# Sums of W2 blocks on GpSimd, and the second tile's row statistics taken later, in a three-stage Perceiver block

## The reference

```
# 1 cross attention
attn = softmax(x1 @ ctx^T); attn /= 1e-9 + attn.sum(rows); x_r = attn @ ctx
t = x1 - (conv_w @ x_r + conv_b);  x1 + relu(batchnorm(t))
# 2 differential attention: 8 heads, Wq, Wk, Wv, Wo of 1024 x 1024
# 3 feed-forward with ternary weights
T(W) = alpha * sign(W) * (|W| > 0.05 * max|W|)      # alpha: mean of the kept |W|
h = gelu(x @ T(W1)^T + b1)                          # 4096 hidden
y = h @ T(W2)^T + b2
out = fake 4 bit quantization of y, scale from max|y|
```

## Time and profile before

| | |
|---|---|
| median of 3 runs | 1398.69 us (1396.48 to 1399.58) |
| the profiled execution | 1399.28 us |
| its span | 1397.5 us |
| mean granted TensorE clock | 0.988 |
| busy: PE, DVE, ACT, POOL | 1353.7, 818.5, 507.7, 2.4 us |

### The profile page before, as it was taken

One profiled execution on the slowest core, in us unless ns is written; L12 is line 12 of the kernel. 1 busy time (PEld: TensorE's weight loads), 2 busy tenths in 40 slices (PEclk: granted clock), 3 DMA queues, 4 the chain that ended last, 5 costly groups with the idle time before them and its releaser, 6 DMA issues.

```text
span 1397.5 us, 17665 instructions
## 1 busy us (share of the span) xinstructions
PE 1353.7 (97%) x6930; PEld 661.3 (47%) x6930; DVE 818.5 (59%) x1405; ACT 507.7 (36%) x786; POOL 2.4 (0%) x10
## 2 busy tenths in 40 slices
PE   6999999999999879999999999999999999999995
PEld 4564645445344334444555555444444444444442
DVE  3242423324233288887888875865677862576874
ACT  1121311113121032117777783002666665333332
POOL 0000000000000000000000000000000000000000
PEclk9999999999999989999999999999999999999998
DMA  9999999999999577755445446342787761222254
GB/s 380 419 421 421 420 422 420 421 421 422 419 393 403 212 295 271 277 203 167 136 131 171 143 143 249 120 147 79 214 237 238 244 196 46 73 79 76 76 173 158
DMA packets 111105, 347.04 MB, mean 248 GB/s; under 512 B 41008, under 2 KB 55728, under 8 KB 85424
## 3 DMA queue, kind: packets, MB, share of 16 engines
q1 hardware_dynamic: 107856, 334.38, 64.9%
q10 hardware_dynamic: 3168, 11.54, 2.0%
HBM read 304.47 MB, written 41.42 MB: 248 GB/s over the span
## 4 chain that ended last, share of the span: by engine, by line
PE 75%; issue 14%; DMA 5%; DVE 5%; ACT 1%; DVEq 0%; POOLq 0%; POOL 0%
PE ps L1062 16%; PE ps L840 13%; PE ps L945 12%; PE ps L1012 8%; PE ps L754 7%; PE ps L899 5%; PE ps L792 4%; PE ps L771 2%; PE ps L774 2%; DMA ctxT<-in_ctxT 2%; PE ps L822 2%; DMA w_scan<-in_w2t 1%; PE ps L965 1%; DMA x_t<-in_x 1%; DVE wmx L1222 1%
## 5 line engine op out<-in xcount | busy, mean ns | idle before, releaser
L1077 PE MATMUL ps<-t_half,hl 128*128 128x512 f16 x896 | 193.5, 379 | 0.0
L840 PE MATMUL ps<-ctx_sb,attnT 128*64 128x512 f32 (+1 forms) x832 | 180.3, 593 | 0.0
L565 ACT ACTIVATE stg<-ps 128x512 f32<-128x512 f32 (+1 forms) x80 | 44.3, 554 | 344.0 <-PE ps L771 173.3
L1077 PEld LDWEIGHTS ps<-t_half,hl 128*128 128x128 f16 x896 | 87.7, 98 | 105.7
L1062 PE MATMUL ps<-x3h,t_buf 128*128 128x512 f16 x512 | 121.0, 379 | 0.0
L1062 PE MATMUL ps<-x3l,t_buf 128*128 128x512 f16 x512 | 121.0, 379 | 0.0
L754 PE MATMUL ps<-ctxT,x1T 128*64 128x512 f32 x512 | 115.4, 595 | 0.9 <-DMA ctxT<-in_ctxT 0.9
L1499 DVE TENSOR_TENSOR hl<-hq,hl 128x512 f16<-128x512 f32 x112 | 76.4, 691 | 66.5 <-ACT hl L696 66.4
L840 PEld LDWEIGHTS ps<-ctx_sb,attnT 128*64 128x64 f32 (+1 forms) x832 | 59.0, 137 | 115.5 <-issue 108.3
L899 PE MATMUL ps<-wv_sb,x2T 128*128 128x512 f32 x256 | 112.4, 597 | 0.0
L1012 PE MATMUL ps<-wo_sb,oT 128*128 128x512 f32 x256 | 111.6, 593 | 0.3 <-ACT oT L645 0.3
(11 more groups left out here) (196 smaller groups left out, 1606.5 us busy)
## 6 DMA issues: line engine op xcount, KB each, us to landing
ctxT<-in_ctxT SPq DMA_DIRECT2D x64, 1024.0 KB, 21.9
ctx_sb<-in_ctx SPq DMA_DIRECT2D x40, 1024.0 KB, 17.3
ctx_sb<-in_ctx SPq DMA_DIRECT2D x8, 4096.0 KB, 27.2
ctx_sb<-in_ctx SPq DMA_DIRECT2D x16, 2048.0 KB, 31.4
w_scan<-in_w1t SPq DMA_DIRECT2D x32, 512.0 KB, 5.9
w_buf<-in_w1t SPq DMA_DIRECT2D x32, 512.0 KB, 3.7
w_scan<-in_w2t SPq DMA_DIRECT2D x32, 512.0 KB, 5.3
w_buf<-in_w2t SPq DMA_DIRECT2D x32, 512.0 KB, 4.0
```

The source lines that it names most:

```text
L840: ins = mm(bank(ea + hf)[C * b:C * b + C, :], attnT[0:w, slots[mt], C * b:C * b + C], ctx_sb[0:w, mt, b, hf * BANK:hf * BANK + BANK], star ...
L1077: ins = mm(bank(b), hl[:, r % RING, n, s * P:s * P + P], t_half[:, r % BRING, :], start=(fresh and k == 0 and n == 0), stop=(k == HK - 1 a ...
```

## The change

Two edits. The four sums of each pair k go from the vector engine's program to GpSimd's, between its reductions of L529 and L531, in the order T3, T1, T2, T4; GpSimd waits for `t2_ready`, and from k = 2 on for the store that frees the set. `stats(1)` goes from ahead of the first tile's pairs to just before the vector engine's copy of pair 4; for later tiles it stays.

```diff
+        p_own = sem("p_own")
...
             pool.partition_all_reduce(wpk[:, 3:4], wpk[:, 1:2], P, RED.max).then_inc(wmax_all, 1)
+            for k in range(HK):
+                B11, B12, B21, B22, T1, T2, T3, T4 = (t2_set[:, k % 2, i, :] for i in range(8))
+                pool.wait_ge(t2_ready, 2 * k + 2)
+                if k >= 2:
+                    pool.wait_ge(t2_stored[k % 2], 16 * (k // 2))
+                pool.tensor_tensor(T3, B22, B12, ALU.subtract).then_inc(p_own, 1)
+                pool.tensor_tensor(T1, B12, B11, ALU.subtract).then_inc(t2_full, 1)
+                pool.wait_ge(p_own, 2 * k + 1)
+                pool.tensor_tensor(T2, T3, B11, ALU.add).then_inc(p_own, 1)
+                pool.wait_ge(p_own, 2 * k + 2)
+                pool.tensor_tensor(T4, B21, T2, ALU.subtract).then_inc(t2_full, 1)
             pool.wait_ge(tot_ready, 2)
...
-                if p + 1 < NT:
+                if 0 < p < NT - 1:
                     stats(p + 1)
                 for e, pair in enumerate(pairs(p)):
+                    if p == 0 and e == 4:
+                        stats(1)
...
                 if n % 2:
                     B11, B12, B21, B22, T1, T2, T3, T4 = (t2_set[:, k % 2, i, :] for i in range(8))
-                    own.done(V.tensor_tensor(T3, B22, B12, ALU.subtract))
-                    own.done(V.tensor_tensor(T2, T3, B11, ALU.add))
-                    V.tensor_tensor(T1, B12, B11, ALU.subtract).then_inc(t2_full, 1)
-                    V.tensor_tensor(T4, B21, T2, ALU.subtract).then_inc(t2_full, 1)
+                    pass
```

## The result

The changed kernel takes 1401.44 us (median of 13 runs, 1399.49 to 1405.35), the kernel before in the same comparison 1398.55 us (13 runs, 1395.83 to 1402.38). The ratio is 1.002, with a 95% interval of 1.0011 to 1.0029: slower by 2.9 us, at the edge of what the forecast called no change. The forecast was 1398.7 us, and 2.9 us are more than the interval leaves to chance, so something is to be explained. In the profiled executions the spans are 1399.6 and 1397.5 us.

The account below looks back on a forecast made before the run. TensorE was taken to bound the kernel, with saturated transfers also deciding in the first part. Statistics 0 us plus sums 0 us left the unchanged kernel's median, 1398.7 us; the range was 1396 to 1418 us.

Parts of the forecast that it names:

- Statistics later: At the start, moving `stats(1)` lets TensorE run up to 3.6 us early, then wait for ctxT: 0 us gained.
- the upper bound of 3.6: At the start, 2.2 us of idling plus 1.4 us of low clock saved, if the transfers moved along.
- the 1.4 us for the low clock: At the start, twelve transposes would take 1.4 us and not 2.8 without TensorE's fall to the lower clock.
- Sums off the vector engine: In the first feed-forward product, 27 us of sums removed beside a TensorE that never idles: worth 0 us.
- Sums on GpSimd: At SP's queue, sums of 1.1 us delay store and t_buf load by 3.0 us, within 6.3 to spare: cost 0.
- Rival A: In the product, GpSimd and vector engine hold each other up: 10.9 us a pair, 12 us stall, 1411 us; chance 0.36.
- 7.6 + 4.8: In the product, 7.6 us of lateness piled up over 14 pairs, plus 4.8 us for seven `sum_1` instructions.
- 6.0: In the product, a pair's sums stretch to 4.4 + 3.3 us against 1.7, so 6.0 us later.
- Rival B: At the start, the 3.6 us saved stay because transfers land earlier: 1395.1 us; chance 0.08.
- C: In the product, a GpSimd sum takes over 2.0 us without any holding up: 1401 us at 2.5 us; chance 0.04.

Follow-up runs that it names:

- half of ctxT: The kernel before with ctxT loaded for only one batch of each tile: 1394.23 us, ratio 0.9968; with the later statistics as well, 1391.96 us, ratio 0.9955.
- shorter load: The kernel before with the last context block loaded without its 63 unused rows: 1415.94 us, ratio 1.0117; with the later statistics as well, 1413.10 us.

## Why the prediction was right or wrong

**What bounds the kernel: right, with a narrow margin in the first stage.** There the transfers lead, but only just: with half of ctxT 4.4 us are gained, and then TensorE is busy 168.00 of 168.00 us from 60 to 228 us, where it was 167.63. In the product it is TensorE: it takes 217.57 us again in four kernels whose vector engine or GpSimd work differs.

**Statistics later, 0 us: right, and shown.** The stall went, waits for the context took its place, and by 55 us nothing was left (ratio 1.0002; a block issued 2.0 us earlier lands no earlier). With lighter transfers a gain is kept, but 2.3 us and not the upper bound of 3.6. Of that bound the 1.4 us for the low clock were mis-sized: they were read from one execution, and another with 2.1 us of idling has none of it. The clock didn't fall in the new waits, which are pieces of 0.2 to 0.8 us.

**Sums off the vector engine, 0 us: nothing speaks against it, but no run tests it by itself.** In every run with the sums on GpSimd the vector engine's other instructions got longer, so that it was never lighter by much (814.7 us busy, not 818.5). The argument is the forecast's: TensorE had no idle time in the product.

**Sums on GpSimd, hidden by 6.3 us at SP: this step failed.** The sums weren't hidden. That the time, 1401.44, still lies within the 1396.5 to 1401.5 forecast for hidden sums is luck. The price was right, 1.1 us taken and 1.15 measured where GpSimd is alone; the condition under which it was used, that both engines stream at once, was not. The step counted 3.0 us of lateness at the tightest t_buf load; it was 10.7. The 3.0 were a misreading too: they set 4.7 us against the 1.7 of the old sums, but in the kernel before the store doesn't wait for the sums. They end at 1129.83, and the store comes at 1131.45, behind the W2 load in SP's queue. These are the kernel before, then the first and last sum of the same pair in the changed kernel, whose store is at 1139.68:

```profile
1127.63 3.78 SPq L485 DMA_DIRECT2D w_buf<-in_w2t  x2
...
1129.41 0.42 DVE L1350 TENSOR_TENSOR t_set<-t_set 128x512 f16<-128x512 f16 x1
...
1131.45 0.43 SPq L489 DMA_DIRECT2D t_dram<-t_set  x1
```

```profile
1132.37 1.53 POOL L536 TENSOR_TENSOR t_set<-t_set 128x512 f16<-128x512 f16 x1 [7.07 <-DVE w_buf L1358]
...
1137.63 2.02 POOL L541 TENSOR_TENSOR t_set<-t_set 128x512 f16<-128x512 f16 x1
```

So 1.6 us more were to spare than the forecast knew. The second pair of the stage shows it: there GpSimd's four sums are undisturbed and end 4.7 us after `t2_ready`, and the store comes 1.6 us later after the product's start than before, not 3.0. The rival with 0.36, A, is what happened, and both experiments with GpSimd beside the kernel before show its cause. The Trainium skill's rule (SBUF — State Buffer, Who interferes with whom) agrees with the rows shown: exclusion for a whole instruction, with two-input vector instructions against GpSimd's reads and not against its writes (1.27 and 1.37 us beside the subtractions, 0.42 beside the memsets). Where I set that rule against "no row shows it", it should have had more than 0.36.

**Rival A's price, 12 us: its terms mis-sized.** Forecast were 12 us of waits and 1411; it came to 2.9 us in the medians (4.7 in the profiled product). The pair's period was forecast as 10.9 us; from the store at 1007.10 to that at 1148.67 there are 13 pairs, 10.89 us each. But only the last of them are made by the streams in a row, as I had it: over the whole stage the vector engine still waits 43.5 us for W2, 2.7 us a pair. For the most part the changed kernel's chain goes round a single W2 buffer:

```profile
1031.87 4.27 DMA w_buf<-in_w2t
...
1036.17 1.77 DVE t_set L1356
...
1037.96 2.06 DVE t_set L1357
...
1041.32 1.16 ACT w_buf L719 x2
...
1042.49 4.10 DMA w_buf<-in_w2t
...
1105.87 0.60 DVE hq L1494
```

Load, three instructions of which two are held up, ScalarE's count, next load: 10.6 us here, each step after the last, and 10.7 on average for the six rounds up to 1096.07. Up to the store at 1103.54 a pair takes 10.72 us. The last four take 11.28: there the vector engine waits for W2 only 4.5 us in all, and the chain goes over a `sum_1` at 1105.87 (L1494) that stands straight ahead of the next L1356. So `sum_1` does cost something there, as A said, but less than its 4.8 us. That the two parts together give A's 10.9 is chance.

At the tightest pair the terms are these, each counted from the product's start. `t2_ready` comes 165.4 us into the product and not 158.7, so 6.7 us late, where A had 7.6 + 4.8. The sums then take 7.3 us against 1.7, so 5.6 more, where A had 6.0, and 1.6 come off for what the store waited before. That is the 10.7. From it comes off the time to spare, 6.3, and 1.3 more since the late load lands in 6.0 us and not 7.3: 3.1 us, and 2.8 were measured. A left out the clock after the stall, 1.7 us.

**Rival B: refuted** for this kernel. **C:** no sum took 2.0 us by itself; those of 2 us in the profile are waits.

No version beat both kernels. With t_buf ahead of the store, or two sums on each engine, the loss is gone, and it stays at no gain, since in the kernel before the vector engine's time isn't on the product's path.

## What to carry to other kernels

Work moved from the vector engine to GpSimd is only off the vector engine if the two don't read at the same time: price it as time of both. Then ask whose queue waits for the slower result, and what stands behind it there; here t_buf loads behind a semaphore were the whole loss, and the order of two lines removed it. Ask as well what the slower result was waiting for already, since that part of the delay is free (1.6 us here). A stall taken out where a saturated queue decides some 35 us later is worth nothing, and the test is whether a block's landing moves with its issue (here issued 2.0 us earlier, landed at 53.3 and 53.2).

## What the runs showed of the hardware

- GpSimd subtracts or adds 128 x 512 f16 in 1.15 us alone, and its memset of that size takes 0.52 us; the vector engine needs 0.42 us for the sum.
- In the profile the wait for the other engine is inside an instruction's duration: 1.23 or 1.28 us became 2.06, 0.42 became 1.27 and 1.37 (1.26 with two sums on each engine). GpSimd's memsets left the two-input sums at 0.42; the one-input L1352 took 2.39 and 1.02 us where it met them, and not 0.75.
- A 65-row transfer of 8 KB rows in a saturated queue made it slower than 128 rows did: 393 against 421 GB/s at the same DMA share, 17.5 us in all for 0.52 MB less a tile. The cause isn't shown.
- TensorE's clock after a stall isn't told by the stall's length alone. In the product the granted clock was 0.59 on average over 3.9 us after 2.42 us of idling, and 0.66 after 2.0 us with the sums alone. Near the start, twelve transposes took 2.82 us after 2.16 us of idling (kernel before) and after 0.91 us (shorter load), both with a granted clock of about 0.5 from 20 to 23 us. They took 1.53 us, with the clock at 1.00, after 2.10 us (sums alone) and after 1.58 us (half ctxT). What decides isn't shown.
